# A sparse-attention block on one core: pair reduction, meeting through PSUM, and the order of the queues

## The reference

```
h = layernorm(x) * (1 + ca) + sa
q, v = relu(h @ enc_q), relu(h @ enc_v)          # 8 heads of 16 dims
m = softplus(base + 0.1 * mlp(mean of q))        # one metric per head and batch
for each head, token t, and the 64 tokens up to t:
    dist = sqrt(sum((k - q)^2 * m) + 1e-8)
    the 32 nearest are kept; w = exp(-dist), normalised over them
    context = w @ v + gate(|q| > 0.2) * 0.1 * (q/|q|) @ (U @ V)
    out = q * context
x = x + ga * (out @ decoder)
h = layernorm(x) * (1 + cb) + sb
x = x + gb * (h + experts(h) weighted by the gates of the batch's first token)
```

## Time and profile before

| what | value |
|---|---|
| median of three runs | 984.59 us |
| profiled execution, its own time | 985.34 us |
| its span, first to last instruction | 983.6 us |
| VectorE busy | 776.1 us (79%) |
| TensorE busy, weight loads | 749.9 us (76%), 497.5 us (51%) |
| GpSimd busy | 520.9 us (53%) |
| ScalarE busy | 498.3 us (51%) |
| mean granted TensorE clock | 0.831 of 2.4 GHz |
| DMA queues, share of 16 engines | under 8% |

### The profile page before, as it was taken

The page is one execution under the profiler, slowest core; times in us unless marked ns, Lnnn a source line. Parts: engine busy times, 40 slices in busy tenths (PEclk is TensorE's granted clock), DMA queues, the critical chain, the costliest instruction groups (busy, mean ns, idle before and its releaser), DMA issues. The chain is left out here.

```text
span 983.6 us, 22709 instructions
## 1 busy us (share of the span) xinstructions
PE 749.9 (76%) x6070; PEld 497.5 (51%) x6133; DVE 776.1 (79%) x5082; ACT 498.3 (51%) x1542; POOL 520.9 (53%) x811
## 2 busy tenths in 40 slices
PE   5877888777778777877777877777777877777876
PEld 3434555545555445554444544455445554544554
DVE  5857899888877887788877788778888788888751
ACT  3962455544555545554455545555445554455532
POOL 2024366556645565565665556656566465665442
PEclk9975787887987988788889779888889798889765
DMA  5300000000000000000000000000000000000000
GB/s 159 97 3 13 14 10 16 17 14 19 18 16 17 16 18 20 15 17 18 16 18 17 16 15 19 19 16 17 17 16 19 16 17 16 17 19 16 18 9 11
DMA packets 41185, 21.22 MB, mean 22 GB/s; under 512 B 6041, under 2 KB 40545, under 8 KB 41057
## 3 DMA queue, kind: packets, MB, share of 16 engines
q1 hardware_dynamic: 41056, 19.77, 7.0%
HBM read 10.44 MB, written 4.19 MB: 15 GB/s over the span
## 5 line engine op out<-in xcount | busy, mean ns | idle before, releaser
L984 DVE MAX8 gsgn_all<-modn_all 128x8 f32<-128x32 f32 x2048 | 204.2, 172 | 0.0
L740 ACT ACTIVATE nst<-psC 16x192 f32<-16x192 f32 x64 | 20.4, 319 | 322.4 <-PE psC L1283 322.4
L1193 PE MATMUL psD<-mask_bf,ident_bf 128*128 128x320 bf16 x256 | 68.5, 412 | 133.9 <-DMA tst<-nst 133.0
L990 DVE MATCH_REPLACE8 modn_all<-gsgn_all,modn_all 128x32 f32<-128x32 f32 x1024 | 166.2, 173 | 0.0
L505 POOL TENSOR_SCALAR n_c<-x,nm_c,rs_c 128x128 f32<-128x128 f32 x64 | 29.1, 454 | 256.9 <-ACT nm_c L678 251.6
L554 POOL TENSOR_TENSOR big<-big,con 128x512 f32<-128x512 f32 x128 | 162.7, 1292 | 4.5 <-DVE big L1033 4.5
L1015 DVE SCALAR_TENSOR_TENSOR key<-psD,key 128x512 f32<-128x512 f32 x64 | 44.2, 691 | 133.5 <-ACT key L701 133.5
L1242 PE MATMUL psC<-vst,big 128*128 128x68 f32 x512 | 107.7, 294 | 0.0
L1193 PEld LDWEIGHTS psD<-mask_bf,ident_bf 128*128 128x128 bf16 x256 | 25.4, 118 | 156.9 <-DMA tst<-nst 144.5
L1243 PE MATMUL psC<-vst,big 128*128 128x68 f32 x512 | 104.4, 287 | 0.0
L1242 PEld LDWEIGHTS psC<-vst,big 128*128 128x128 f32 x512 | 82.6, 203 | 19.0 <-issue 18.5
(11 more groups left out here) (212 smaller groups left out, 1767.7 us busy)
## 6 DMA issues: line engine op xcount, KB each, us to landing
tst<-qT_all SPq DMA_DIRECT2D x256, 17.0 KB
big<-in_x SPq DMA_DIRECT2D x16, 256.0 KB, 3.1
xs<-in_x SPq DMA_DIRECT2D x64, 64.0 KB, 1.9
out<-yo SPq DMA_DIRECT2D x64, 64.0 KB, 1.6
sst<-nst SPq DMA_DIRECT2D x128, 3.0 KB
tst<-nst SPq DMA_DIRECT2D x128, 2.0 KB
con<-in_consts SPq DMA_DIRECT2D x1, 581.5 KB, 5.9
wmod_sb<-in_wmod SPq DMA_DIRECT2D x1, 384.0 KB, 4.4
```

The source lines that it names most:

```text
L984: last = v.max(top[:, u, h, where], low_high[:, u, h])
L990: last = v.match_replace(low_high[:, u, h], top[:, u, h, 0:8], low_high[:, u, h], GONE)
L1193: mm(bank_of(r)[:, :, 0:PW], ident_bf[:], mask_bf[:].unsqueeze(1).broadcast_to([P, NG, PW]), start=True, stop=False, skip_group_check=True)
```

## The change

- **SyncE.** In `step` the output DMA moves from the front to the end, behind the row DMAs and the x DMA.
- **GpSimd.** `n_c` (L505) moves behind `sqs` and `sst`.
- **VectorE.** The three operations that form the pairs become two TENSOR_REDUCE over a strided view, one of them with `negate`. At the meeting the sign change and the maximum become two instructions, the first with its result in PSUM (`pHigh`, in the bank of pDT and pZ). `den` moves in front of L1015 and `rden` in front of `drop(1)`.
- **ScalarE.** The order within a step changes: mean and deviation, lnn and rnn, q and key, cst, the two signs, vst, nst, n2, h2T, x2, ln and the first exp, yo, oT, and last the second exp. `n2` is taken one step later. In front of vst stand waits for the norm matmuls.
- **TensorE.** The order within a step changes: C, the diff's transposes, values, `pN`, `pNN`, count, `pN2`, attention, masks and distances, the key's transposes, y, o. `pN` and `pNN` lie in the first bank of psW. The waits of gate rows and of C on `n2` go; the key's transposes wait for `nst` and `n2`. The three matmuls of `keep_clock` on psC stand behind the wait for vst and in front of the one for wab.

```diff
@@ -227,9 +227,10 @@
         pQH = pH[:, :, QH0:B0]
         pXT, pV = psW[:, 0], psW[:, 0]
         pDT, pZ = psW[:, 1], psW[:, 1]
+        pHigh = psW[:, 1, 0:2 * NH * 8].rearrange("p (h n) -> p h n", h=NH)
         pC = psC[:, 0:8 * VP]
-        pN = psC[0:2 * NH, 8 * VP:8 * VP + 3 * WIN]
-        pNN = psC[:, 8 * VP + 3 * WIN:8 * VP + 3 * WIN + NH]
+        pN = psW[0:2 * NH, 0, 3 * WIN:6 * WIN]
+        pNN = psW[:, 0, 6 * WIN:6 * WIN + NH]
         pN2 = psX[:, 0:P]
         pY = psX[:, P:2 * P]
         pO = psX[:, 2 * P:3 * P]
@@ -308,6 +309,7 @@
...
@@ SyncE, step @@
-                k = i - 4
-                if there(k):
-                    sync.wait_ge(yo_ready, k + 1)
-                    sync.dma_start(oc[:, k], yo[:, k % 2]).then_inc(out_in[k % 2], 16)
...
+                k = i - 4
+                if there(k):
+                    sync.wait_ge(yo_ready, k + 1)
+                    sync.dma_start(oc[:, k], yo[:, k % 2]).then_inc(out_in[k % 2], 16)
...
@@ ScalarE, step: two waits and the norm copies @@
+                need(act, pnn_ready, min(i + 3, NCH))
+                need(act, pn_ready, min(i + 4, NCH))
...
+                k = i + 3
+                if there(k):
+                    s = k % 2
+                    need(act, rows_in[s], ROWS_IN * (k // 2))
+                    nc.scalar.activation(nst[:, s], pN, ACT.Copy).then_inc(nst_ready, 1)
+                k = i + 2
+                if there(k):
+                    need(act, gat_ready, k - 3)
+                    need(act, rnn_ready, k - 3)
+                    nc.scalar.activation(n2[:, k % 4], pNN, ACT.Copy, scale=-2.0).then_inc(n2_ready, 1)
...
@@ VectorE, step @@
-                    x4 = key[:, i % 2].rearrange("p (h u j) -> p h u j", h=NH, u=2)
+                    x4 = key[:, i % 2].rearrange("p (h u j) -> p h j u", h=NH, u=2)
                     dve.wait_ge(d2_ready, i + 1)
                     need(dve, theta_ready, i)
-                    v.tensor_tensor(low_high[:, 1], x4[:, :, 0], x4[:, :, 1], ALU.max).then_inc(pair_done, 1)
-                    v.tensor_tensor(low_high[:, 0], x4[:, :, 0], x4[:, :, 1], ALU.min).then_inc(pair_done, 1)
-                    dve.wait_ge(pair_done, 3 * i + 1)
-                    v.tensor_scalar(low_high[:, 1], low_high[:, 1], -1.0, None, ALU.mult).then_inc(pair_done, 1)
-                    dve.wait_ge(pair_done, 3 * i + 2)
+                    v.tensor_reduce(low_high[:, 0], x4, AX_X, ALU.min).then_inc(pair_done, 1)
+                    v.tensor_reduce(low_high[:, 1], x4, AX_X, ALU.max, negate=True).then_inc(pair_done, 1)
+                    dve.wait_ge(pair_done, 2 * i + 1)
                     pick(0, 0)
-                    dve.wait_ge(pair_done, 3 * i + 3)
+                    dve.wait_ge(pair_done, 2 * i + 2)
...
-                    v.scalar_tensor_tensor(out=meet, in0=top[:, 1], scalar=-1.0, in1=top[:, 0], op0=ALU.mult,
+                    need(dve, w_ready, i)
+                    v.tensor_scalar(pHigh, top[:, 1], -1.0, None, ALU.mult).then_inc(high_done, 1)
+                    dve.wait_ge(high_done, i + 1)
+                    v.scalar_tensor_tensor(out=meet, in0=pHigh, scalar=0.0, in1=top[:, 0], op0=ALU.max,
                                            op1=ALU.max).then_inc(meet_done, 1)
...
@@ TensorE, step @@
+                k = i - 2
+                if there(k):
+                    blk = 2 * (k % CPB)
+                    if k == 0:
+                        pe.wait_ge(gb_ready, 2)
+                    pe.wait_ge(vst_ready, 2 * k + 2)
+                    need(pe, cst_ready, 2 * k)
+                    keep_clock(psC, PW, 3)
+                    pe.wait_ge(wab_ready, 2 * k + 2)
+                    for r in range(4):
+                        cols = slice(r * P, (r + 1) * P)
+                        o = pC[:, r * 2 * VP:(r + 1) * 2 * VP].rearrange("p (v x) -> p v x", v=2)
+                        mm(o, wab[:, k % 2, 0, cols], vst[:, blk + 1:blk + 3, r], start=True, stop=False)
+                        last = mm(o, wab[:, k % 2, 1, cols], vst[:, blk:blk + 2, r], start=False, stop=True)
+                    last.then_inc(c_ready, 1)
+
                 k = i - 1
                 if there(k):
-                    pe.wait_ge(ln_done, min(k + 2, NCH))
+                    pe.wait_ge(diff_ready, k + 1)
+                    need(pe, w_ready, k)
+                    for r in range(4):
+                        last = nc.tensor.transpose(pDT[:, r * P:(r + 1) * P], diff[:, r * P:(r + 1) * P], ident)
+                    last.then_inc(dT_ready, 1)
+
+                need(pe, ln_done, min(i + 1, NCH))
+                k = i - 1
+                if there(k):
                     for n, blk in enumerate(new_blocks(k)):
                         c0 = (k // CPB) * TP + blk * WIN
                         for a in range(2):
                             last = mm(pV[a * WIN:(a + 1) * WIN, n * WIN:(n + 1) * WIN], hT_all[:, c0:c0 + WIN], encv_a[:, a],
                                       start=True, stop=True)
                     last.then_inc(v_ready, 1)
-
-                    pe.wait_ge(diff_ready, k + 1)
-                    need(pe, w_ready, k)
-                    for r in range(4):
-                        last = nc.tensor.transpose(pDT[:, r * P:(r + 1) * P], diff[:, r * P:(r + 1) * P], ident)
-                    last.then_inc(dT_ready, 1)
-
-                k = i - 2
-                if there(k):
-                    blk = 2 * (k % CPB)
-                    if k == 0:
-                        pe.wait_ge(gb_ready, 2)
-                    pe.wait_ge(n2_ready, min(k + 5, NCH))
-                    keep_clock(psC, PW, 3)
-                    pe.wait_ge(wab_ready, 2 * k + 2)
-                    pe.wait_ge(vst_ready, 2 * k + 2)
-                    for r in range(4):
-                        cols = slice(r * P, (r + 1) * P)
-                        o = pC[:, r * 2 * VP:(r + 1) * 2 * VP].rearrange("p (v x) -> p v x", v=2)
-                        mm(o, wab[:, k % 2, 0, cols], vst[:, blk + 1:blk + 3, r], start=True, stop=False)
-                        last = mm(o, wab[:, k % 2, 1, cols], vst[:, blk:blk + 2, r], start=False, stop=True)
-                    last.then_inc(c_ready, 1)
+                k = i + 3
+                if there(k):
+                    need(pe, n2_ready, k - 1)
+                    pe.wait_ge(opnd_ready, k + 1)
+                    for g in range(NG):
+                        last = mm(pN, selm[:, k // CPB, g], sqs[:, g], start=(g == 0), stop=(g == NG - 1))
+                    last.then_inc(pn_ready, 1)
+                k = i + 2
+                if there(k):
+                    pe.wait_ge(nst_ready, k + 1)
+                    mm(pNN, nst[:, k % 2, WIN:3 * WIN], con[0:2 * NH, C_ID + NH:C_ID + 2 * NH], start=True,
+                       stop=True).then_inc(pnn_ready, 1)
...
+                    pe.wait_ge(nst_ready, min(k + 3, NCH))
+                    pe.wait_ge(n2_ready, min(k + 2, NCH))
```

More of the change, by code:

```diff
@@ L518, in step @@
                                             ALU.mult).then_inc(s_ready, 1)
+                k = i - 4
+                if there(k):
+                    pool.wait_ge(nm_done, k + 1)
+                    pool.wait_ge(rs_done, k + 1)
+                    need(pool, pn2_ready, k - 1)
+                    nc.gpsimd.tensor_scalar(n_c[:, k % 2], x2[:, k % 2], nm_c[:, k % 2:k % 2 + 1], rs_c[:, k % 2:k % 2 + 1],
+                                            ALU.add, ALU.mult).then_inc(nc_ready, 1)
                 k = i + 1
@@ L732, in step @@
                     nc.scalar.activation(x2[:, k % 2], pAtt, ACT.Copy).then_inc(x2_ready, 1)
[L734 to L740, removed]
                 k = i + 1
@@ L751, in step @@
                     nc.scalar.activation(e, e, ACT.Exp, scale=0.5).then_inc(root_done, 1)
[L752 to L762, removed]
                 k = i - 4
@@ L774, in step @@
                     nc.scalar.activation(oT[:, k % 2], pO, ACT.Copy).then_inc(oT_ready, 1)
-                k = i + 3
+                k = i + 1
                 if there(k):
[L778 to L781, removed]
+                    e = infl[:, k % 2]
+                    act.wait_ge(root_done, k + 1)
+                    nc.scalar.activation(e, e, ACT.Exp, scale=-1.0).then_inc(infl_ready, 1)
             steps(step, routing)
@@ L1009, in step @@
                         expert_matrices(1)
-                k = i + 1
-                if there(k):
-                    dve.wait_ge(outer_ready, k + 1)
-                    e = key[:, k % 2].rearrange("p (h j) -> p h j", h=NH)
-                    v.scalar_tensor_tensor(out=e, in0=pB, scalar=0.0, in1=e, op0=ALU.max, op1=ALU.min).then_inc(d2_ready, 1)
-                if there(i):
-                    dve.wait_ge(picked, 6 * i + 2)
-                    drop(1)
                 k = i - 2
@@ L1026, in step @@
                     v.tensor_scalar(den[:, s], cst[:, s, :, HD], 1e-8, None, ALU.add).then_inc(den_done, 1)
+                k = i + 1
```

(31 more changed lines are left out.)

55 lines of the change are left out of this document (31 added, 24 removed).

## The result

The changed kernel takes **735.38 us** (median of four runs, 729.82 to 737.28); the kernel before, with a fourth run beside the three of above, 984.76. The ratio is 0.7456, with a 95% interval of 0.7408 to 0.7504. One execution of experiment 9 ran in a slower state of the chip, 1.6% above the fastest of its kernel, and is left out of that median and ratio.

A forecast was written before the change was run, and what follows sets the result against it. The ring through the output DMA was taken as the bound, VectorE next. VectorE's 4.86 + 2.85 + 2.1 + 0.62 = 10.43 us per step, against 13.51, saved 194 us over 63 steps: 790 us, range 742 to 872.

The forecast's parts named there:

- The ring through the output DMA: Output DMA, row DMAs, masks, key transposes, ScalarE's yo, next output DMA: claimed to set the period, 13.41 us.
- VectorE next: VectorE's own work, 11.3 us per step before the edits, was claimed to bound once its 2.10 us wait went.
- 4.86 for the work between the joining of the key and the pairs: VectorE from L1015 to the pairs: 6.16 us less 1.30 for the old meeting.
- 2.85 for picks and drops: VectorE's work between the pairs and L1015, claimed at 2.85 us per step.
- 0.62 for the meeting: VectorE's two 128-element operations through PSUM with a hand-over: 0.62 us, bounds 0.5 and 0.9, gain 0.68.
- The pairs: VectorE's two new strided reduces: 1.10 us each, 2.1 together with overlap, in place of 2.29.
- rival (a): VectorE's two new reduces run at the dense price: step 9.73 us, 747 us in all; chance 0.16.
- part 2: Forming the pairs on VectorE by two reduces: gain 0.2 to 0.9 us per step, 0.2 taken.
- part 1: Reordering queues and norm rows, output DMA behind row and x DMAs: opens the ring, taking 2.10 us per step from VectorE.
- (b): TensorE becomes the bound at its present mixture of clocks: 10.9 us per step, 821 us; chance 0.16.
- (d): Slower: TensorE stays at half clock, 15.5 us per step, 1111 us; chance 0.04.
- rival (c): GpSimd holds up VectorE's new reduces by 1.41 us, or a new wait that size: step 11.84, 880 us; chance 0.16.

The follow-up runs named there:

- experiment 9: The changed kernel with the meeting's sign change given to ScalarE and VectorE forming the next step's pairs meanwhile: 707.60 us, ratio 0.7196.
- experiments 1: The kernel before with the two VectorE edits alone (reduces for the pairs, meeting through PSUM): 982.81 us, ratio 0.998.
- 2: The kernel before with one edit, SyncE issuing the output DMA last in its step: 863.95 us, ratio 0.8779.
- 5: The changed kernel with one edit, SyncE issuing the output DMA first in its step again: 818.39 us, ratio 0.8316.
- experiment 7: The changed kernel with reduces that nobody reads added in VectorE's drain, in various strides and groupings; 256 elements took 405 ns at step 2, 590 at 4.
- experiment 4: The changed kernel with only the old pairs put back, 842.59 us, and with only the old meeting put back, 757.73 us.
- experiment 8: The changed kernel without its six matmuls without a reader, 757.85 us, and without only the three in front of C, 745.81 us.
- experiment 6: The kernel before with the output DMA last and the two VectorE edits, all other orders kept: 804.11 us, ratio 0.8170.

## Why the prediction was wrong, and where it was right

- **The bound before, right.** The ring through the output DMA set 13.41 us; experiments 1 (0.998) and 2 (0.8779) show it from both sides, and 5 brings it back. Its removal was priced at the 2.10 us that VectorE waited; alone it brought 13.51 - 11.61 = 1.90. Not said there: the round holds work at 1.2 GHz, for each of the 63 steps of the kernel before has a stretch at it, 4.2 us on average; in the changed kernel 3 steps have one.
- **VectorE next, right.** It is at 98%, and the sum of its step was right but for one term: 9.46 measured, 10.43 forecast. 4.86 for the work between the joining of the key and the pairs: measured 464.19 - 458.79 - 0.65 = 4.75. 2.85 for picks and drops: measured 458.79 - 455.94 = 2.85, den included. 0.62 for the meeting: measured 463.80 - 463.15 = 0.65.
- **The pairs, the step that failed.** I priced 2.1 us, from L816's 1.88 ns per element; they take 1.21. 0.89 us too much, 63 times, are 56 us: 790 - 56 = 734, the measured time within 2 us. The prediction had named the dense price as rival (a), and even that was too high with 1.4: the two durations are 0.69 and 0.68, but the second starts 0.61 us after the first. L816 was the nearest row in name and the wrong one in kind: its elements each open a new place, while the pairs go on by one element in two places, which experiment 7 shows to be free. The row L1015, 512 elements in 0.69 us, was the one to take. The range stopped at 742 because its low end rested on the same 1.4.
- **What the pairs replace, mis-sized too.** 2.29 us was read in the old order; in the new one they would take 3.02. That made no error in the sum, which used the new operations only, but the gain of 0.2 us that I gave to part 2 is 107 us in all (experiment 4).
- **The rest of the reordering, not seen.** I treated part 1 as one and gave its parts no prices of their own. Opening the ring needs the output DMA alone (121 us). The other parts are worth 69 us more once the VectorE edits are in: they open a second ring of 9.78 us, and with them 3 of 63 steps have a stretch at the low clock instead of 19. The sum did not need this ring, since the changed kernel had it open.
- **TensorE, right.** 8.4 us at full clock was the estimate; 181.91 us in 200 are 8.7 us per 9.55, at clock 1.00, with gaps of 0.8 us in front of C. Rivals (b) and (d) did not come. That they could have, experiment 8 shows: I had counted the six matmuls only as a cost of up to 1.1 us; without them the kernel is 22 us slower.
- **No blocked reduce, right** (683/698/702 ns beside GpSimd's diff): rival (c) is out.

## What to carry to other kernels

Follow the longest wait of the busiest engine until it comes back to itself; if the round takes exactly one period, work saved outside it is worth nothing (0.998) and one moved DMA may be worth half of everything. A mean period can be a mixture of two kinds of step (9.78 and 12.4 us in experiment 6): look at the single intervals and their clock before you look for a ring of the mean's length. When an operation is missing from the trace, choose the row that matches its order of addresses, not its name, and keep a range that reaches past the cheaper row's price with overlap. In a kernel that is near two bounds, the price of an operation depends on what runs beside it in the *new* order.

## What the runs showed of the hardware

- A float32 VectorE reduce of 256 elements takes 405 ns at steps 1 and 2, 457 to 486 at 3, 568 to 618 at 4, 8 and 16. Two alternating places are free if each goes on by one element (422 for 256, 674 for 512), eight are not (576).
- Beside GpSimd's operations with two SBUF inputs a one-input tensor_scalar from SBUF to SBUF went from 0.28 to 0.92 us; the same kind with its result in PSUM stayed at 294/295/296 ns.
- Behind a wait of 1.54 us TensorE ran 3.7 us of work near 1.2 GHz (granted clock 0.56) in the kernel without the matmuls that nobody reads. With them, and waits of 0.8 us in front of C, the granted clock was 1.00 from 140 to 500 us, although they produce nothing.
